# Paired first chunks, projection from columns, and the feature product behind the graph

## The chip, the cores and the metric

One core of a Trainium2 chip runs the whole program in one launch. The metric is device time in microseconds. The kernel before took 1318.92 us (median of three runs, 1317.95 to 1318.94).

## The reference

x is 4096x128, adj is 4096x4096 (values 0 or positive), all in fp32. Two layers follow each other, each with its residual and a layer norm over the 128 features.

```
A = adj without its diagonal, d = its diagonal
ns = A @ x                                   # node support
edge = gru(ns, x);  es = mean over 3 heads of gat(x, A)
node = gru(es, x)
x1 = layernorm(x + d * edge + d * node)
h2 = tanh(x1 @ W_proj + b_proj)
x2 = layernorm(x1 + relu(F @ (h2 @ W_gcn) + b_gcn)),  F = tanh(adj * adj) where adj > 0
```

A head of gat sums masked columns into scores, takes a softmax over each row of A and multiplies it by A and by x @ W. The top 350 entries of a row of F are all its entries here, since a row holds far fewer.

## The kernel before

The columns are cut into 8 chunks of 512, each chunk into 8 pieces: four 128x512 tiles of the transposed adjacency, 1 MB. All big products have their result in columns (features on the 128 partitions, 512 nodes on the free axis). Each engine runs its list of instructions in the written order; semaphores (wait_ge) tie them. Three stages follow each other.

**Support stage** (lines 130 to 520). The sync engine (SP) loads pieces into a ring of 5, and a load waits until TensorE, VectorE (mask) and ScalarE (sign count) are through with the piece five earlier. In chunk 0 each piece has its 256 KB of x loaded ahead of it, and the whole 2 MB of transposed x follows piece 7. TensorE makes ns (L427): four fp32 products a piece. Every fp32 product of the kernel stands in the trace as two records.

**Middle stage** (L1450 to L1830). For each of 256 tiles n (chunk c, k from 0 to 31): VectorE and ScalarE make gaps (L1723, L1614), ScalarE one exponential over three heads (L1621), VectorE the product with the adjacency (L1737), TensorE three products (L1821). Six buffers hold such terms. ScalarE's order in iteration n is gap(n+1), exp(n), and then what stands there for this n. At k = 8 TensorE combines the heads of the chunk before (L1788), and ScalarE takes that out at k = 12 (L1603).

**Tail** (L963 to L1443). For each chunk the gates of both cells run on TensorE (L1313, L1315: twelve 512-column products), ScalarE reads them (L1083, L1087, L1091) and makes n (L1095), VectorE makes the cells (L1175 to L1191) and adds them (add_cells, L1198). TensorE turns the sum into rows (turn_cells, L1324); VectorE multiplies by the diagonal and adds x (make_y, L1204), measures (L1211, L1214), GpSimd computes the inverse root (L1043 to L1055), VectorE normalizes (finish_x, L1218). TensorE turns the rows back (turn_x, L1332), multiplies by W_proj (project, L1339), ScalarE applies tanh (make_h2, L1107), TensorE multiplies by W_gcn (features, L1346), ScalarE copies (L1111). Then the graph product runs over 64 pieces: VectorE squares a piece (square_a, L1226), ScalarE takes tanh (L1115), TensorE does four products (graph, L1374). Three of the squares stand inside the gate chunks (0, 3 and 5). A chunk's features leave over ScalarE's relu (L1122), transposes (turn_features, L1385), VectorE's addition (L1236) and the second norm. The last 128 columns are done apart, in row form (L1371), with a single VectorE step behind them (L1232). Orders of the tail before:

```
ACT, chunk c: read_hid e, read_r e, read_z e, [tanh], h2(c-3), make_n e, read_hid n, read_r n, copy_x(c-2), read_z n, make_n n, copy_g(c-3)
DVE, chunk c: pre_n e, finish_x(c-2), make_y(c-1), measure(c-1), cell e, [square], pre_n n, cell n, add_cells(c)
PE,  chunk c: gates e, project(c-3), turn_cells(c-1), gates n (turn_x(c-2) inside), features(c-3)
```

Of the kernel before, what the change touches and what calls it, by code (L numbers as in the profile page):

```python
# [73 lines left out]

def piece_of(n):


    c, g = divmod(n, NPIECE)
    return c, (g + {0: 1, NCHUNK - 1: NCHUNK - 1}.get(c, 0)) % NPIECE
# [8 lines left out]
def loads_of(n):  # L88


    return 16 * (n // RING + (1 if n % RING else 0))


def wait_piece(engine, loaded, cleared, n):

    c, g = piece_of(n)
    if g == c:
# [41 lines left out]
def support_phase(nc, sem, dram, keep):  # L139
# [6 lines left out]
    x_ready = [sem(f"a_x{s}") for s in range(RING)]  # L146
    exps, parts_made, small = sem("a_exps"), sem("a_parts"), sem("a_small")
    loaded = [sem(f"a_loaded{s}") for s in range(RING)]
    first_loaded = [sem(f"a_first_loaded{j}") for j in range(PIECE)]
# [7 lines left out]
    with ExitStack() as ctx:  # L157
# [33 lines left out]

        def sync_program(sp):
            for n in range(NPIECE):
                tiles = slice((n + 1) % NPIECE * PIECE, ((n + 1) % NPIECE + 1) * PIECE)
# [4 lines left out]
                sp.dma_start(x_sb[:, tiles, :], dram["x_p"][:, tiles, :]).then_inc(x_ready[n % RING], 16)  # L199
                if n:  # L200
                    load_piece(sp, dram, pieces, loaded, n)
                else:
                    for j in range(PIECE):
                        sp.dma_start(pieces[:, 0, j, :], dram["adj_c"][0, :, PIECE + j, :]).then_inc(first_loaded[j], 16)
                if n == UV_AFTER:
                    sp.dma_start(x_t, dram["x_t"]).then_inc(x_t_ready, 16)
            for n in range(NPIECE, NPIECES):
                sp.wait_ge(masked, n - RING + 1)
                sp.wait_ge(signed, n - RING + 1)
                sp.wait_ge(ns_done, n - RING + 1)  # L210
                load_piece(sp, dram, pieces, loaded, n)
# [12 lines left out]
        def scalar_program(act):  # L224
            def count_below(n):
                if n:
                    wait_piece(act, loaded, cleared, n)
# [5 lines left out]
            def ns_take_out(c):  # L233
                b, out = c % 2, ns_sb[c % 2][:, :] if c < NCHUNK - 1 else last_ns
                act.wait_ge(ns_done, NPIECE * (c + 1))
# [14 lines left out]

            for j in range(PIECE):
                act.wait_ge(first_loaded[j], 16)
# [7 lines left out]
            for n in range(NPIECES):  # L260
                count_below(n)
                c, g = divmod(n, NPIECE)
                if c and g == 0:
                    ns_take_out(c - 1)
                if c and g == 2:
# [10 lines left out]
        def vector_program(dve):  # L276
            nc.vector.memset(ones[:, :], 1.0).then_inc(filled, 1)
            nc.vector.memset(wide_ones[:, :], 1.0).then_inc(filled, 1)
            nc.vector.memset(uv_parts[:, :, :], 0.0).then_inc(filled, 1)
            nc.vector.memset(w6[:, :], 0.0).then_inc(folded_out, 1)  # L280
            dve.wait_ge(filled, 3)
            nc.vector.memset(uv_parts[:, :, 0:1], 1.0).then_inc(filled, 1)

            def make_mask(n):
                c, g = piece_of(n)
                if n:
                    wait_piece(dve, loaded, cleared, n)
                else:
                    for j in range(PIECE):
                        dve.wait_ge(first_loaded[j], 16)  # L290
# [24 lines left out]
            for n in range(MASKS_FIRST):  # L315
                make_mask(n)
                if n == UV_AFTER - 2:
                    dve.wait_ge(folded, 1)
                    dve.wait_ge(folded_out, 1)
                    nc.vector.tensor_copy(w6[:, 0:NUV], w6_ps).then_inc(folded_out, 1)  # L320
                if n == UV_AFTER:
# [15 lines left out]
            for n in range(MASKS_FIRST, NPIECES):  # L337
                make_mask(n)
                c, g = divmod(n, NPIECE)
                if c and g == (4 if c < NCHUNK - 1 else NPIECE - 2):  # L340
                    make_e(c - 1)
# [74 lines left out]
        def tensor_program(pe):  # L416
            def ns_products(n, first=0, end=PIECE):
                c, g = piece_of(n)
                at = n % NPIECE
                if at == 0 and first == 0 and c >= 2:  # L420
                    pe.wait_ge(ns_out, c - 1)
                if n:
                    wait_piece(pe, loaded, cleared, n)
                for j in range(first, end):
                    if n == 0:
                        pe.wait_ge(first_loaded[j], 16)
# [5 lines left out]
            def pos_products(c, first=0, end=NPIECE):  # L432

                pe.wait_ge(masked, NPIECE * c + end)
# [4 lines left out]
                for i in range(first * PIECE, end * PIECE):  # L439
                    q, k = i % CHUNK, piece_of(NPIECE * c + i // PIECE)[1] * PIECE + i % PIECE  # L440
# [19 lines left out]

            for n in range(UV_AFTER + 1):
# [2170 lines left out]
```

## Time and profile before

| | |
|---|---|
| profiled execution | 1318.72 us, span 1317.1 us |
| support / middle / tail | 0 to 257, 257 to 981, 981 to 1317 us |
| PE / DVE / ACT / POOL busy | 99% / 77% / 71% / 8% |
| granted TensorE clock | 1.00 of full speed throughout |

The busy share says which engine has work nearly always. In the timelines, a record's "idle before" names what the engine waited for. TensorE's records overlap, so a stretch is best read from the start of one group to the start of the next.

### The profile page before, as it was taken

The page shows a single profiled execution, that of the slowest core. Times are in us where ns is not written, and L with a number is a line of the kernel's source. Part 1 is how long each engine was busy: PE and PEld are TensorE (multiplying, and loading weights), DVE is VectorE, ACT ScalarE, POOL GpSimd, SP SyncE. Part 2 cuts the span into 40 slices and gives each one's busy share as a digit, 9 for nine tenths or more (in the row PEclk, how much of TensorE's full clock was granted, in tenths as well). Part 3 has the DMA queues.
Part 4 walks back from the last instruction along what each step waited for, and adds up shares of the span by engine and source line. Part 5 has one row for each costly group of instructions (what it writes and reads, how often), then busy time and mean ns, then how long its engine had stood idle before and what let it go on. Part 6 is the DMA issues. An engine that isn't in the chain of part 4 may idle for free.

```text
span 1317.1 us, 12199 instructions
## 1 busy us (share of the span) xinstructions
PE 1304.8 (99%) x4203; PEld 590.0 (45%) x4203; DVE 1009.5 (77%) x1427; ACT 936.3 (71%) x950; POOL 102.5 (8%) x188
## 2 busy tenths in 40 slices
PE   8999999999999999999999999999999999999998
PEld 3444444444444444444444444444444555444445
DVE  2433333457998998999989999899868988678885
ACT  4655555338988899889889899898945556545563
POOL 0100001000100100100100100100003562000000
PEclk9999999999999999999999999999999999999999
DMA  9988888263233242232323423322113437888880
GB/s 367 355 291 287 281 296 295 79 238 127 84 139 130 95 146 96 97 143 97 145 99 116 152 96 122 118 96 96 64 62 129 144 115 252 296 307 294 302 285 18
DMA packets 46712, 228.95 MB, mean 174 GB/s; under 512 B 10611, under 2 KB 16436, under 8 KB 21044
## 3 DMA queue, kind: packets, MB, share of 16 engines
q1 hardware_dynamic: 44082, 225.55, 48.6%
q10 hardware_dynamic: 2562, 2.56, 0.6%
q8 instruction: 35, 0.57, 0.2%
q14 instruction: 33, 0.27, 0.1%
HBM read 223.80 MB, written 4.29 MB: 173 GB/s over the span
## 4 chain that ended last, share of the span: by engine, by line
PE 96%; DMA 2%; DVE 1%; issue 0%; SPq 0%; POOL 0%; ACT 0%; POOLq 0%
PE t_y_ps L1821 49%; PE ns_ps L427 15%; PE t_y_ps L1374 13%; PE rows_ps L1374 4%; PE t_y_ps L1799 3%; PE t_y_ps L1313 3%; PE t_y_ps L1315 2%; DMA pieces<-in_adj_c 2%; PE t_es_ps L1788 2%; PE pos_ps L441 1%; PE rows_ps L1315 1%; PE t_y_ps L1371 1%; PE t_es_ps L1346 1%; PE t_y_ps L1339 1%; DVE mask L1737 0%
## 5 line engine op out<-in xcount | busy, mean ns | idle before, releaser
L1821 PE MATMUL t_y_ps<-mask,x_sb 128*128 128x512 f32 x1536 | 662.6, 592 | 0.2 <-DVE mask L1737 0.2
L1821 PEld LDWEIGHTS t_y_ps<-mask,x_sb 128*128 128x128 f32 x1536 | 290.6, 190 | 366.0 <-issue 350.0
L1737 DVE TENSOR_TENSOR mask<-mask 128x1536 f32<-128x1536 f32 x256 | 450.1, 1759 | 0.2 <-ACT mask L1621 0.2
L1621 ACT ACTIVATE mask<-mask,ones 128x1536 f32<-128x1536 f32 x256 | 399.7, 1562 | 0.0
L1614 ACT ACTIVATE mask<-mask,pieces 128x512 f32<-128x512 f32 x352 | 241.5, 712 | 35.0 <-PE t_y_ps L1821 32.8
L427 PE MATMUL ns_ps<-pieces,x_sb 128*128 128x512 f32 x504 | 226.5, 602 | 6.8 <-DMA pieces<-in_adj_c 6.6
L1723 DVE TENSOR_SCALAR mask<-mask,e_cols 128x512 f32<-128x512 f32 x416 | 189.0, 487 | 50.6 <-PE t_y_ps L1821 44.2
L1115 ACT ACTIVATE mask<-mask 128x2048 f32<-128x2048 f32 x64 | 121.7, 1909 | 80.5 <-DVE mask L1226 80.0
L1374 PE MATMUL t_y_ps<-mask 128*128 128x512 f32 x384 | 167.0, 592 | 0.1
L427 PEld LDWEIGHTS ns_ps<-pieces,x_sb 128*128 128x128 f32 x504 | 93.8, 192 | 123.0 <-issue 116.6
L291 DVE TENSOR_SCALAR mask<-pieces 128x2048 fp8e4<-128x2048 f32 x64 | 76.8, 1224 | 93.1 <-DMA pieces<-in_adj_c 75.2
L1226 DVE SCALAR_TENSOR_TENSOR mask<-mask 128x2048 f32<-128x2048 f32 x64 | 142.2, 2282 | 0.8 <-DMA mask<-in_adj_c 0.8
L230 ACT ACTIVATE signs<-pieces 128x2048 fp8e4<-128x2048 f32 x64 | 122.3, 1911 | 26.2 <-DMA pieces<-in_adj_c 12.5
L1374 PEld LDWEIGHTS t_y_ps<-mask 128*128 128x128 f32 x384 | 72.3, 190 | 87.8 <-issue 86.6
L1575 POOL TENSOR_TENSOR mask<-mask,off_diag 128x128 f32<-128x128 f32 x32 | 30.8, 991 | 686.0 <-DMA mask<-in_adj_c 686.0
L1374 PE MATMUL rows_ps<-mask 128*128 128x512 f32 (+1 forms) x128 | 48.8, 539 | 0.0
L1313 PE MATMUL t_y_ps<-pieces 128*128 128x512 f32 x96 | 46.5, 593 | 0.0
L305 DVE TENSOR_SCALAR e_scl<-e_ps 128x128 f32<-128x128 f32 x8 | 2.3, 291 | 54.0 <-PE e_ps L453 54.0
L1799 PE MATMUL t_y_ps<-mask,pieces 128*32 128x512 fp8e4 x768 | 42.5, 379 | 0.0
L1236 DVE TENSOR_TENSOR x_sb<-t_y_ps,x_sb 128x512 f32<-128x512 f32 (+1 forms) x8 | 5.4, 675 | 42.1 <-PE t_y_ps L1385 42.1
L1374 PEld LDWEIGHTS rows_ps<-mask 128*128 128x128 f32 x128 | 24.2, 190 | 23.3 <-issue 15.1
L241 ACT COPY ns_sb<-ns_ps 128x512 f32<-128x512 f32 x7 | 4.1, 583 | 41.2 <-PE ns_ps L427 41.2
(177 smaller groups left out, 614.5 us busy)
## 6 DMA issues: line engine op xcount, KB each, us to landing
mask<-in_adj_c SPq DMA_DIRECT2D x128, 1024.0 KB, 4.8
pieces<-in_adj_c SPq DMA_DIRECT2D x63, 1024.0 KB, 5.0
mask<-scratch_shifts SPq DMA_DIRECT2D x8, 1536.0 KB, 7.3
x_sb<-in_x_p SPq DMA_DIRECT2D x8, 256.0 KB, 9.9
mask<-in_x_t SPq DMA_DIRECT2D x1, 2048.0 KB, 16.8
pieces<-in_x_t SPq DMA_DIRECT2D x8, 256.0 KB, 3.0
pieces<-scratch_ns_t SPq DMA_DIRECT2D x8, 256.0 KB, 3.6
scratch_ns_t<-ns_sb ACTq DMA_DIRECT2D x7, 256.0 KB, 5.9
```

What stands on the lines that cost most here:

```text
L230: nc.scalar.activation(signs[:, :], pieces[:, n % RING, :, :].rearrange("p k n -> p (k n)"), ACT.Relu, scale=-1.0, saturate=False, accum_o ...
L427: mm = nc.tensor.matmul(ns_ps[c % 2][:, :], x_sb[:, g * PIECE + j, :], pieces[:, n % RING, j, :], start=at == 0 and j == 0, stop=at == NPI ...
L1115: nc.scalar.activation(piece(u), piece(u), ACT.Tanh).then_inc(filtered, 1)
L1226: nc.vector.scalar_tensor_tensor(piece(u), piece(u), 0.0, piece(u), ALU.max, ALU.mult).then_inc(squared_a, 1)
L1313: mm = nc.tensor.matmul(gate_ps[g][:, :], whh[k][:, at:at + H], x_t[c % 2], start=True, stop=g == "hid_n")
L1374: mm = nc.tensor.matmul(f_ps[i % len(f_ps)][:, q * P:end * P], g_all[:, k, :], piece(u)[:, j * CW + q * P:j * CW + end * P], start=k == 0, ...
L1614: last = nc.scalar.activation(term(n)[:, h, :], shift_of(c)[:, 0, h, :], ACT.Relu, bias=minus_e[:, k, 1 + h:2 + h])
L1621: nc.scalar.activation(t, t, ACT.Exp, bias=ones[:, :], scale=-1.0).then_inc(exped, 1)
L1723: last = nc.vector.tensor_scalar(term(n)[:, h, :], shift_of(c)[:, 0, h, :], e_cols[:, k, 1 + h:2 + h], 0.0, ALU.subtract, ALU.max)
L1737: nc.vector.tensor_tensor(term(n), term(n), a, ALU.mult).then_inc(terms, 1)
L1799: mm = nc.tensor.matmul(sums_ps[g % 2][s * LINES:(s + 1) * LINES, :], parts[:, k, h, :], mask[:, c, k, :], start=k == 0, stop=k == NB - 1)
L1821: mm = nc.tensor.matmul(y_ps[c % 2][h][:, :], x_sb[:, k, :], term(n)[:, h, :], start=k == 0, stop=k == NB - 1)
```

## The change

**Head.** The pieces of chunks 0 and 1 come in pairs, (0,2), (1,2), (0,3), (1,3) and so on, the four with the diagonals last; a 256 KB part of x goes with each piece of chunk 0 only. The first two pieces are loaded and consumed by tile, the first part of x goes on ScalarE's queue, and transposed x comes in eight parts, one each behind pieces 8 to 15. TensorE begins with seven products of zeros. The scores' uv product stands behind piece 16, and pos_products, sum_e and turn_e of chunks 0 and 1 inside chunk 2.

**Tail.** The sum of the cells is multiplied by the diagonal and x is added while still in columns (make_y); that tile is turned into rows for the norm and also projected directly, with W_proj centered beforehand (center_weights, at tile (5, 10) of the middle stage, read out there by ScalarE). The norm's root and b_proj come in afterwards (scale_h). turn_x, copy_x and features go away. The graph product takes h2, and the product with W_gcn stands behind it (feed, in turn_features' place), the bias and relu with it on VectorE. The last 128 columns take this same way. The diagonal is loaded as rows, chunk by chunk; SP loads the first two ahead of the tail's first pieces and waits for all 24 y_scaled.

```
ACT, chunk c: read_hid e, read_r e, read_z e, [tanh], make_n e, read_hid n, copy_rows(c-1), read_r n, h2(c-2), read_z n, make_n n
DVE, chunk c: pre_n e, scale_h(c-2), measure_y(c-1), cell e, [square], pre_n n, cell n, make_y(c)
PE,  chunk c: gates e, turn_cells(c-1), gates n (project(c-1) inside)
```

```diff
+FIRST = [(c, g) for g in range(2, NPIECE) for c in range(2)] + [(c, g) for c in range(2) for g in range(2)]
+X_WITH = [n for n, (c, g) in enumerate(FIRST) if c == 0]
...
+    if n < len(FIRST):
+        return FIRST[n]
...
-UV_AFTER = NPIECE - 1
+BY_TILE = 2
+WARM = 7
+UV_AFTER = 2 * NPIECE
...
+            for n in range(NPIECES):
...
+                if n in X_WITH and n:
+                    load_x(sp, n)
+                if n >= BY_TILE:
                     load_piece(sp, dram, pieces, loaded, n)
                 else:
                     for j in range(PIECE):
...
+                if NPIECE <= n < NPIECE + NCHUNK:
+                    cols = slice((n - NPIECE) * CW, (n - NPIECE + 1) * CW)
+                    sp.dma_start(x_t[:, cols], dram["x_t"][:, cols]).then_inc(x_t_ready, 16)
...
+            load_x(act, 0)
...
+            pe.wait_ge(filled, 1)
+            zeros = uv_parts[:, :, :].rearrange("p t j -> p (t j)")
+            for i in range(WARM):
+                nc.tensor.matmul(e_t_ps[:, :], zeros[:, 0:P], zeros[:, 0:CW], start=True, stop=True)
...
+CENTER_AT = (5, 10)
...
+        nc.vector.tensor_scalar(center, ident[:, :], 1.0 / H, None, ALU.subtract).then_inc(bias_step, 1)
...
+        nc.tensor.matmul(bank[:, 0:H], center, w_proj, start=True, stop=True).then_inc(centered, 1)
...
+        act.wait_ge(centered, 1)
+        nc.scalar.copy(w_center, bank[:, 0:H]).then_inc(center_out, 1)
...
+        def copy_rows(c):
+            act.wait_ge(turned, c + 1)
+            nc.scalar.copy(x1[:, rows(c), :].rearrange("p r f -> p (r f)"), cell_ps[c % 2][:, :]).then_inc(rows_copied, 1)
...
+            act.wait_ge(scaled, CHUNK * (c + 1))
+            nc.scalar.activation(g_all[:, rows(c), :].rearrange("p r f -> p (r f)"), pre_h[c % 2], ACT.Tanh).then_inc(copied, 1)
...
             make_n("edge", c)
             read_hid("node", c)
+            if c:
+                copy_rows(c - 1)
             read_r("node", c)
             if c >= 2:
-                copy_x(c - 2)
+                make_h2(c - 2)
...
+            nc.vector.tensor_tensor(both, cell["edge"], cell["node"], ALU.add).then_inc(y_step, 1)
...
+            nc.vector.tensor_tensor(both, both, diag_rows[c % 2], ALU.mult).then_inc(y_step, 1)
...
+            nc.vector.tensor_tensor(both, both, x_t[c % 2], ALU.add).then_inc(cells, 1)
+
+        def scale_h(c):
+            dve.wait_ge(rooted, POOL_STEPS * (c + 1))
+            dve.wait_ge(projected, c + 1)
...
+                nc.vector.scalar_tensor_tensor(pre_h[c % 2][:, q * P:(q + 1) * P], h_ps[c % 2][:, q * P:(q + 1) * P], root[:, t:t + 1], b_proj,
+                                               ALU.mult, ALU.add).then_inc(scaled, 1)
...
+        def measure_y(c):
+            dve.wait_ge(rows_copied, c + 1)
+            measure(rows(c), stats, moments, stats_made, averaged)
...
             pre_n("edge", c)
             if c >= 2:
-                finish_x(c - 2)
+                scale_h(c - 2)
             if c:
-                make_y(c - 1)
-                measure(rows(c - 1), stats, moments, stats_made, averaged)
+                measure_y(c - 1)
             make_cell("edge", c)
...
+            if g == 3:
+                finish_x(c - 1)
...
+                mm = nc.tensor.matmul(h_ps[c % 2][:, q * P:(q + 1) * P], both[:, q * P:(q + 1) * P], w_center, start=True, stop=True)
...
+                mm = nc.tensor.matmul(back_ps[i % 2][:, t * P:(t + 1) * P], feat_t[i % 2][:, t * P:(t + 1) * P], w_gcn,
+                                      start=i not in BIAS_FIRST, stop=True)
...
-            if c >= 3:
-                project(c - 3)
             if c >= 1:
                 turn_cells(c - 1)
             pe.wait_ge(es_out, c + 1)
...
-            sp.wait_ge(y_scaled, HEADS * (NCHUNK - 1))
+            sp.wait_ge(y_scaled, HEADS * NCHUNK)
+            for c in range(2):
+                load_diag(sp, c)
             sync_tail(sp)
...
+                if (c, k) == CENTER_AT:
+                    keep_center(act, rows_ps)
...
+                    if (c, k) == CENTER_AT:
+                        pe.wait_ge(shifts_out, NGROUP)
+                        center_weights(pe, rows_ps)
```

## Rows read from the trace of the kernel before

**Rows 1.** The page: busy time of the engines, and the costliest group.
```profile
PE 1304.8 (99%) x4203; PEld 590.0 (45%) x4203; DVE 1009.5 (77%) x1427; ACT 936.3 (71%) x950; POOL 102.5 (8%) x188
...
L1821 PE MATMUL t_y_ps<-mask,x_sb 128*128 128x512 f32 x1536 | 662.6, 592 | 0.2 <-DVE mask L1737 0.2
```

**Rows 2.** Timeline (start, length, engine, line), the first 45 us, TensorE.
```profile
4.77 6.15 PE L427 MATMUL ns_ps<-pieces,x_sb 128*128 128x512 f32 x8 [4.77 <-DMA pieces<-in_adj_c]
12.73 14.38 PE L427 MATMUL ns_ps<-pieces,x_sb 128*128 128x512 f32 x32 [1.80 <-DMA pieces<-in_adj_c]
...
34.84 3.67 PE L427 MATMUL ns_ps<-pieces,x_sb 128*128 128x512 f32 x8 [0.20 <-POOL pieces L222]
```

**Rows 3.** Timeline, chunk 5 around tile 10 of the middle stage, ScalarE and VectorE.
```profile
742.66 1.56 ACT L1621 ACTIVATE mask<-mask,ones 128x1536 f32<-128x1536 f32 x1
...
752.33 0.59 ACT L1603 COPY mask<-t_es_ps 128x512 f32<-128x512 f32 x1 [2.84 <-PE t_es_ps L1788]
752.82 1.33 ACT L1614 ACTIVATE mask<-mask,pieces 128x512 f32<-128x512 f32 x2
...
755.71 1.75 DVE L1737 TENSOR_TENSOR mask<-mask 128x1536 f32<-128x1536 f32 x1
```

**Rows 4.** Windows (length, busy by engine, clock, DMA share, GB/s), a gate stretch.
```profile
1050.00:1100.00 50.00, 50.00 (x169) 26.02 (x168) 40.92 (x94) 25.61 (x37) 28.85 (x60) 1.00 0.45 160
```

**Rows 5.** Timeline, one chunk of the gates, VectorE.
```profile
1061.49 0.69 DVE L1180 SCALAR_TENSOR_TENSOR pieces<-pieces,rows_ps 128x512 f32<-128x512 f32 x1
1062.09 1.11 DVE L1218 TENSOR_SCALAR x_sb<-x_sb,h_moments,h_root 128x128 f32<-128x128 f32 x4
1063.12 1.12 DVE L1204 SCALAR_TENSOR_TENSOR x_sb<-t_y_ps,diag,x_sb 128x128 f32<-128x128 f32 x4
...
1065.34 0.66 DVE L1187 TENSOR_TENSOR pieces<-pieces 128x512 f32<-128x512 f32 x1
...
1073.50 0.69 DVE L1180 SCALAR_TENSOR_TENSOR pieces<-pieces,rows_ps 128x512 f32<-128x512 f32 x1 [0.41 <-PE rows_ps L1315]
```

**Rows 6.** Timeline, the same chunk, TensorE's turn_cells.
```profile
1061.16 0.60 PE L1324 MATMUL t_y_ps<-ident,pieces 128*128 128x128 f32 x4
```

**Rows 7.** Timeline, the same chunk, ScalarE.
```profile
1062.60 0.72 ACT L1095 ACTIVATE pieces<-pieces,h_bias 128x512 f32<-128x512 f32 x1
1063.21 0.69 ACT L1083 ACTIVATE pieces<-t_y_ps,h_bias 128x512 f32<-128x512 f32 x1
```

**Rows 8.** Timeline, first and last steps of the gates, SP's queue and VectorE.
```profile
981.50 1.28 SPq L1060 DMA_DIRECT2D mask<-in_adj_c  x3
...
981.58 1.89 DVE L1711 TENSOR_TENSOR mask<-t_y_ps,mask 128x512 f32<-128x512 f32 x3 [7.96 <-PE t_y_ps L1821]
...
986.29 2.29 DVE L1226 SCALAR_TENSOR_TENSOR mask<-mask 128x2048 f32<-128x2048 f32 x1 [0.79 <-DMA mask<-in_adj_c]
...
998.79 0.68 DVE L1175 SCALAR_TENSOR_TENSOR pieces<-pieces 128x512 f32<-128x512 f32 x1
...
1084.10 0.69 DVE L1198 TENSOR_TENSOR pieces<-pieces 128x512 f32<-128x512 f32 x1
```

**Rows 9.** Timeline, from the last gate to the steady graph product.
```profile
1091.32 0.36 DVE L1214 BATCH_NORM_AGGREGATE h_moments<-h_stats 128x2 f32<-128x6 f32 x4
...
1099.86 1.11 DVE L1218 TENSOR_SCALAR x_sb<-x_sb,h_moments,h_root 128x128 f32<-128x128 f32 x4 [3.80 <-POOL h_root L1055]
...
1106.36 1.90 ACT L1115 ACTIVATE mask<-mask 128x2048 f32<-128x2048 f32 x1
...
1108.40 16.98 PE L1374 MATMUL t_y_ps<-mask 128*128 128x512 f32 x39
```

**Rows 10.** Timeline, the end.
```profile
1294.80 0.67 ACT L1122 ACTIVATE pieces<-t_y_ps,pieces 128x512 f32<-128x512 f32 x1
...
1296.32 0.69 DVE L1236 TENSOR_TENSOR x_sb<-t_y_ps,x_sb 128x512 f32<-128x512 f32 x1 [3.36 <-PE t_y_ps L1385]
...
1312.14 0.29 DVE L1232 SCALAR_TENSOR_TENSOR x_sb<-t_y_ps,x_sb 128x128 f32<-128x128 f32 x1 [2.33 <-PE t_y_ps L1371]
```

More of the change, by code:

```diff
@@ L474, in tensor_program @@
             last.then_inc(uv_t_done, 1)
-            for n in range(UV_AFTER + 1, NPIECE + 1):
-                ns_products(n)
+            ns_products(UV_AFTER + 1)
             pe.wait_ge(uv_t_out, 2)
@@ L913, in load_small @@
                                  ).then_inc(keep["small_loaded"], 16)
+        if not diagonal:
+            return
         engine.dma_start(keep["diag"][:, :], dram["adj"].rearrange("a b -> (a b)")[0:N * N:N + 1]
@@ L1277, in vector_tail @@
             make_cell("node", c)
-            add_cells(c)
+            make_y(c)
         end = NCHUNK - 1
-        finish_x(end - 1)
+        scale_h(end - 1)
         square_a(3)
-        make_y(end)
-        measure(rows(end), stats, moments, stats_made, averaged)
+        measure_y(end)
         square_a(4)
         square_a(5)
-        finish_x(end)
+        scale_h(end)
         for u in range(6, NPIECE):
@@ L1291, in vector_tail @@
             c, g = divmod(u, NPIECE)
+            if g == 3:
+                finish_x(c - 1)
+            if c == end and g == 6:
+                finish_x(end)
             if c < end and g == 5:
@@ L1403, in tensor_tail @@
             gate("node", "r", c)
-            if c >= 2:
-                turn_x(c - 2)
+            if c == 1:
+                pe.wait_ge(center_out, 1)
+                pe.wait_ge(es_out, NCHUNK)
+            if c >= 1:
+                project(c - 1)
             gate("node", "z", c)
             gate("node", "in_n", c)
-            if c >= 3:
-                features(c - 3)
         end = NCHUNK - 1
-        project(end - 2)
         graph(0, 0)
@@ L1414, in tensor_tail @@
         turn_cells(end)
-        turn_x(end - 1)
-        features(end - 2)
-        graph(2, 0)
-        project(end - 1)
-        graph(3, 0)
-        features(end - 1)
-        graph(4, 0)
-        turn_x(end)
-        graph(5, 0, tiles=range(0, 2))
         project(end)
-        graph(5, 0, tiles=range(2, PIECE))
-        features(end)
-        end = (NCHUNK - 1) * NPIECE
-        for u in range(6, end):
+        for u in range(2, end * NPIECE):
             c, g = divmod(u, NPIECE)
@@ L1431, in tensor_tail @@
             if c and g == 2:
-                turn_features(c - 1)
-        for u in range(end, NPIECES):
-            graph(u, NCHUNK - 1, 0, CHUNK - 1)
-            if u == end + 4:
-                turn_features(NCHUNK - 2)
-        for u in range(end, NPIECES):
-            graph(u, NCHUNK, CHUNK - 1, CHUNK)
-            if u == end + 1:
-                turn_features(NCHUNK - 1)
-    return load_weights, load_in, make_biases, sync_tail, pool_tail, scalar_tail, vector_tail, tensor_tail
+                feed(c - 1)
+        last = len(END_PARTS) - 1
+        for u in range(end * NPIECE, NPIECES):
+            graph(u, end, 0, CHUNK - 1)
+            if u == end * NPIECE + 4:
+                feed(end - 1)
+        bias_first(last)
+        for u in range(end * NPIECE, NPIECES):
+            graph(u, last, CHUNK - 1, CHUNK)
+            if u == end * NPIECE + 1:
+                feed(end)
+        feed(last)
+    return load_weights, load_in, load_diag, make_biases, center_weights, keep_center, sync_tail, pool_tail, scalar_tail, vector_tail, tensor_tail
 def on_dve(k):
```

291 lines of the change are left out of this document (137 added, 154 removed).

## The prediction

> **What bounds the kernel now.** I read the page first: TensorE is busy 99% of the span, at 0.43 us a record (662.6 us over 1536) [rows 1], so a change gains what it takes off TensorE, unless it makes TensorE wait. Then the timelines, stretch by stretch, for how far the other engines are ahead. The reader is to see three places. At the start TensorE waits for loads: its first eight records take 6.15 us where eight later take 3.67, the second piece starts at 12.73, the next four pass at about 3.6 us each, and only from 34.84 is it never starved [rows 2]. In the middle stage ScalarE is four tiles ahead [rows 3], a lead that hides any short stop. In the gates TensorE is full, 50.0 of 50.0 us [rows 4], but VectorE waits for it only 0.41 us in a chunk of 12.01 us, from 1061.49 to 1073.50 [rows 5]: there the two are level, and work added to VectorE is not free.
>
> The sum is made against the profiled execution, 1318.7 us, 0.2 below the median of the runs.
>
> **Head.** A piece needs 8 records, 3.44 us, on TensorE. Before, each came with 1.25 MB, at 3.6 us a piece. In pairs it is 1.125 MB, 3.25 us at the same rate: TensorE becomes the slower one from the third piece. That piece lies behind 3.5 MB and not 3.75 MB of loads. Two pieces end now at 12.73 + 3.6 = 16.3; the third could be multiplied at about 15.5, and some 0.5 us earlier because the first x goes on another queue: 15.0. Then five pieces (17.2) and the small folding product (0.7) put the eighth at 32.9, against 34.84 [rows 2]: -1.9. Bounds: -0.5, if tile loads (eight issues ahead of the third piece) eat the lead, and -4, if only TensorE's own two pieces at full rate limited it. The seven products of zeros run while nothing has landed, at no cost, and spare the first pieces the slow rate; that is inside -1.9, since the second piece's landing decides. The transposed x, 0.25 MB behind each of eight pieces, is covered: a load is issued five pieces (17 us) ahead of its use. Moved pos_products, sum_e and turn_e are the same instructions with as many pieces around them: 0.
>
> **Middle: one step with one wait.** center_weights is 2 records of 128 columns, 0.22 us at four records in 0.44 (the length of the turn less its drain, 0.60 - 0.16) [rows 6]. But keep_center stands at the same tile (5, 10) in ScalarE's list as the product in TensorE's, and ScalarE waits for it. ScalarE's exponential of tile 170 ends at 744.22; the copy L1603, which stands behind the exponential of tile 172, waited 2.84 us for the combination behind tile 168 and did so without harm, as four tiles lay ready [rows 3]. TensorE ends that combination at 752.3, tiles 169 and 170 at 752.3 + 2 x 2.58 = 757.4, the centering at 757.7. Only now does ScalarE copy (0.3), make two gaps of tile 172 (1.24 from start to start of what follows [rows 3]), and the exponential of tile 171 (1.56); VectorE multiplies (1.75) [rows 3]; with hand-overs of 0.05 TensorE gets tile 171 at 762.7. All buffers have run dry: 5.0 us idle and 0.2 for the product, and 0.1 for the thin lead behind it: +5.3. Queued behind the waiting ScalarE instruction are all its gaps and exponentials, so both other engines stop. Bounds: 0.2, if ScalarE were less far ahead than counted, and 6.
>
> The trace shows TensorE's first eight records at 6.15 us instead of 3.44, behind an idle start, though the granted clock reads 1.00 of 2.4 GHz [rows 2, 4]. A second idle stretch of 5 us could bring that rate back: 6.15 - 3.44 = 2.7 us more. The Trainium skill (TensorE: Matmul & The Clock Gate, Why this matters for your kernels) says that a long enough gap between bursts of matmuls brings half rate back; by it the total would be 2.7 higher. No gap in this trace is long enough to test it.
>
> **Start of the tail.** SP now waits for VectorE's last scaling, 981.58 + 1.89 = 983.5, where the first pieces went out at about 981.5, and issues two broadcasts of the diagonal first: the first piece goes out 2.9 us later. VectorE's square of it stands between two gate steps at 986.29, when it landed [rows 8]; it comes at about 989.2, less 0.5 that VectorE already waited behind it for TensorE: +2.4. With two more additions to make_y of chunk 0, chunk 1 starts not at 998.79 but 3.0 to 3.9 later; the node half finds TensorE's results ready and takes back nearly 1: +2.9.
>
> **Gates.** TensorE loses turn_x (0.44), features (8 records of 128 columns, 0.89) and swaps project's two long records (0.86) for eight short (0.89): 12.93 us a chunk become 11.6, 1.3 x 8 = 10.4 us less. VectorE decides instead. Its chunk is 12.01 - 0.41 = 11.60. Out go finish_x (1.03) and the old make_y (about 1.15), together with measure (1.07) the stretch from 1062.09 to 1065.34 [rows 5]. In come scale_h, four instructions with a PSUM operand as the old make_y (1.15), and two 512-column operations more (0.69 each, 0.72 apart: 1.44): 12.0. Then a new wait. measure_y needs copy_rows, which needs the turn, which needs make_y, VectorE's last step of the chunk before. Count from the first pre_n: scale_h ends at 2.5. The turn is done at 0.8, but in ScalarE's list copy_rows stands behind make_n of the edge cell, which VectorE releases at 1.4 (two steps of 0.7), and read_hid: 1.44 + 0.61 [rows 7] + 0.58 = 2.6, copy 0.6 (as L1603 [rows 3]), so 3.25: VectorE waits 0.8. The chunk is 12.8, in chunk 1 too, which has no scale_h to fill the wait. The squares of chunks 3 and 5 (2.2 net of overlap each) lie on VectorE as before. Seven chunks: 7 x 12.8 + 4.4 = 94.0 against 1084.79 - 998.79 = 86.0 [rows 8]: +8.0. With +2.9 the last cell is made at 1095.7, 10.9 late, and TensorE waits about 1 us a chunk in turn_cells, with the node gates queued behind it. Bounds for the gates: -10.4 (all of TensorE's saving) to +12.
>
> **From gates to graph.** From 1095.7: scale_h(6) 1.15, square 2.2, tanh 1.9, copy_rows(7) 0.6 behind it, measure 1.1: 1102.7. GpSimd's root took 1099.83 - 1091.68 = 8.1 [rows 9]: 1110.8. scale_h(7) 1.15, square of piece 6 2.3, its tanh 1.9: 1116.2, while TensorE did pieces 0 to 5 from 1090.9 on. Before, piece 6 started at 1108.40 [rows 9]: +7.8. From there TensorE (3.44 a piece) is the slower again: VectorE has 2.2 a piece, and about 25 us in 27.9 a chunk; the later finish_x and bias additions (1.1 + 0.7) bring that to 27.
>
> **End.** feed has two records a tile where the transposes had one: 31 x 0.11 = 3.4, and the last tile. That one is on the path: after the graph's last product VectorE started at once at 1312.14; now ScalarE copies 128 columns (0.3; 0.67 is 512 of them [rows 10]), TensorE multiplies, VectorE follows. Relu to addition took 1296.32 - 1294.80 = 1.52 for four tiles [rows 10], so about 0.95 for one: +1.0. The bias row's product only changes place. Tail in all: 7.8 + 3.4 + 1.0 = 12.2.
>
> The copy stands behind a square root here. The Trainium skill (ScalarE: Activation LUTs, Table sets: the hidden batching unit) has copy in every table set, thus no reload; if not, two loads would be added. No row shows a copy behind a square root.
>
> **Sum.** 1318.7 - 1.9 + 5.3 + 12.2 = 1334.3; with the 0.2 to the median 1334.5 us.
>
> **Rivals.**
> (1) TensorE alone decides: the gates keep their VectorE slack and ScalarE's stop is hidden. -1.9 + 0.2 - 10.4 + 3.4 + 1.0 = -7.7: 1311.2 us, faster. For it: TensorE is 99% busy [rows 1] and loses 7 us net. Against: VectorE waited for it only 0.41 us a chunk [rows 5]. Should the stop at (5, 10) remain, it is 1316.3. It decides if VectorE's chunk is under 11.6.
> (2) Tail as forecast, the stop hidden (5.1 less): 1329.4. Against: ScalarE's tile 171 cannot start before the copy.
> (3) The stop as forecast, but copy_rows ready in time, seven times 0.8 less: 1328.9.
> (4) The forecast and half rate after the stop: 1337.2, the slowest of them. For it, the first records' rate [rows 2].
>
> **Chances.** Forecast 0.45; (1) in both forms 0.1; (2) 0.08; (3) 0.12; (4) 0.25. The range 1326 to 1341 holds all but the first, with errors of a few us in the counted waits. A change under 0.2% (2.6 us) is about what a measurement can't tell from none: faster 0.09, same 0.03, slower 0.88.
>
> **What would show it.** TensorE idle about 5 us behind tile (5, 10), released by VectorE's L1737 behind an exponential behind the center copy. VectorE idle 0.8 us a chunk ahead of bn_stats, released by ScalarE's copy; gate chunks of 12.8 us; turn_cells with TensorE idle ahead of it. Piece 6 of the graph about 8 us later than the head and middle shifts give. The eighth piece 2 us earlier. The prediction is wrong if TensorE stays full through (5, 10), or if gate chunks come at 11.6 to 12.

## The result, and the profile after

The changed kernel takes 1345.41 us (median of 5 runs, 1344.19 to 1348.10), the kernel before 1317.95 (5 runs beside it): a ratio of 1.0209, 95% interval 1.0198 to 1.0220. It is slower, as forecast, but 10.9 us slower than the forecast of 1334.5 and outside its range. The profiled execution of it took 1348.1 us, the slowest of the five; its span is 1346.8, 29.7 longer than before. Of the executions in the experiments one, of experiment 10, took 2322.54 us at a mean clock of 0.557; without it that kernel's median is 1337.95 us, with it 1338.17. I take the profiled span apart from start to end.

**Head.** Timeline of TensorE, start:

```profile
1.45 3.10 PE L492 MATMUL e_t_ps<-uv_parts 128*128 128x512 bf16 x7 [1.45 <-DVE ones L306]
5.19 7.21 PE L455 MATMUL ns_ps<-pieces,x_sb 128*128 128x512 f32 x16 [0.64 <-DMA x_sb<-in_x_p]
13.78 10.57 PE L455 MATMUL ns_ps<-pieces,x_sb 128*128 128x512 f32 x24 [1.37 <-DMA pieces<-in_adj_c]
24.18 0.73 PE L500 MATMUL end_ps<-a_sb,w_t 128*128 128x2 f32 x6
24.77 11.40 PE L455 MATMUL ns_ps<-pieces,x_sb 128*128 128x512 f32 x26
```

The seven products of zeros (L492) end before the first load is there. Two pieces are done at 12.4, the third starts at 13.78, and from there TensorE is full, the small folding product (L500) included: the eighth piece is reached at 24.77 + 16 x 0.43 = 31.7 where it was 34.84 [rows 2]. The whole stage stays 3.4 us ahead.

**Middle.** ScalarE, VectorE and TensorE around tile (5, 10), then windows (length, busy by engine, granted clock, DMA share, GB/s):

```profile
754.32 0.27 ACT L1095 COPY pieces<-rows_ps 128x128 f32<-128x128 f32 x1 [13.48 <-PE rows_ps L1091]
...
757.31 1.76 DVE L1773 TENSOR_TENSOR mask<-mask 128x1536 f32<-128x1536 f32 x1 [9.11 <-ACT mask L1655]
...
759.12 6.46 PE L1857 MATMUL t_y_ps<-mask,x_sb 128*128 128x512 f32 x11 [4.84 <-DVE mask L1773]
```
```profile
758.00:760.00 2.00, 0.88 (x1) 0.50 (x2) 2.00 (x4) 2.00 (x3) 0.00 (x0) 0.67 0.00 0
760.00:762.00 2.00, 2.00 (x4) 0.83 (x3) 1.92 (x2) 2.00 (x3) 0.00 (x0) 0.50 0.92 291
762.00:764.00 2.00, 2.00 (x6) 0.93 (x5) 1.44 (x1) 2.00 (x3) 0.00 (x0) 0.97 0.55 234
```

ScalarE stood 13.48 us ahead of a copy of 0.27, its lead of four tiles [rows 3] was gone, and TensorE waited 4.84 us. Then the granted clock fell to 0.50, which is 1.2 GHz, and TensorE lost another 1.6 us. The stage costs 6.8.

**Start of the tail and gates.** SP's queue and VectorE at the start; then TensorE in the gates of chunk 4, and the windows of that stretch:

```profile
986.95 0.80 SPq L1068 DMA_DIRECT2D mask<-in_diag  x2
987.79 1.52 SPq L1120 DMA_DIRECT2D mask<-in_adj_c  x3
```
```profile
994.98 2.29 DVE L1282 SCALAR_TENSOR_TENSOR mask<-mask 128x2048 f32<-128x2048 f32 x1 [6.07 <-DMA mask<-in_adj_c]
...
1007.22 0.68 DVE L1220 SCALAR_TENSOR_TENSOR pieces<-pieces 128x512 f32<-128x512 f32 x1
```
```profile
1041.14 1.88 PE L1372 MATMUL t_y_ps<-pieces 128*128 128x512 f32 x4
...
1049.64 1.11 PE L1383 MATMUL t_y_ps<-ident,pieces 128*128 128x128 f32 x4 [3.19 <-DVE pieces L1249]
1050.55 3.62 PE L1372 MATMUL t_y_ps<-pieces 128*128 128x512 f32 x4
```
```profile
1049.00:1051.00 2.00, 1.36 (x5) 1.25 (x6) 1.97 (x4) 0.05 (x1) 0.00 (x0) 0.50 0.13 39
1051.00:1053.00 2.00, 2.00 (x3) 0.67 (x2) 0.95 (x4) 1.11 (x2) 0.00 (x0) 0.50 0.85 277
1053.00:1055.00 2.00, 2.00 (x4) 0.85 (x3) 1.25 (x9) 0.72 (x2) 0.01 (x1) 0.50 0.74 151
1055.00:1057.00 2.00, 2.00 (x12) 1.25 (x11) 1.93 (x4) 1.13 (x2) 1.82 (x3) 0.84 0.92 386
```

The first square starts at 994.98 where it was 986.29 [rows 8], and chunk 1 at 1007.22 where it was 998.79: 8.4 later, 5.0 of them made here. From 1007.22 the seven chunks and the last cell take until 1108.80, 101.6 us where they took 86.0: +15.6. A chunk without a square, with TensorE at full clock, takes 12.83 (1021.63 to 1034.46), as forecast. But behind the waits of 2.63, 3.19 and 3.17 us TensorE runs four records in 3.6 us instead of 1.88. The granted clock is at 0.50 for about 3 us in the first case and nearly 7 in the other two. As the node gates of that chunk lie in this stretch, VectorE waits for them: the chunks that begin so take 14.41, 15.67 and 15.69 us and not 12.83, together 7.3 us more. The other two long ones, 15.05 and 15.02, are the plain chunk and a square. In a second profile of the same kernel (experiment 9) the three chunks take 14.44, 14.08 and 14.41 us, together 4.4 more: the waits are the same, the price of the clock behind them is not.

**Graph and end.** TensorE:

```profile
1129.41 19.10 PE L1407 MATMUL t_y_ps<-mask 128*128 128x512 f32 x40 [2.22 <-ACT mask L1168]
...
1323.63 1.16 PE L1426 MATMUL t_y_ps<-pieces 128*128 128x128 f32 x8 [2.36 <-ACT pieces L1175]
1324.62 7.91 PE L1407 MATMUL rows_ps<-mask 128*128 128x384 f32 x24
...
1341.31 0.49 PE L1426 MATMUL t_y_ps<-pieces 128*128 128x128 f32 x2 [0.35 <-ACT pieces L1175]
```

Piece 6 starts 21.0 later than before [rows 9], less than the last cell (24.0 later), about as forecast. Its 40 records then take 19.10 and not 17.40, behind a wait of 2.22. The feeds cost 3.6 (0.45 for each of the first six, 0.55 and 0.34 for the two behind them). In the last chunk, whose records have 384 columns, TensorE waits 2.36 for VectorE, which costs 2.5, and the end is 0.9 longer. Head -3.4, middle +6.8, start +5.0, gates +15.6, up to piece 6 -3.0, from there +8.7: 29.7.

### The profile page after: what moved, and what is told of

Its sections match the earlier page's. It is cut to its first block, busy times and chain, and to the rows that moved or that the text cites. A ratio compares the mean times of both kernels' runs of the same rounds, so it can differ in the third digit from the quotient of the medians.

```text
span 1346.8 us, 12227 instructions
## 1 busy us (share of the span) xinstructions
PE 1312.2 (97%) x4197; PEld 591.9 (44%) x4197; DVE 1026.3 (76%) x1452; ACT 931.2 (69%) x944; POOL 97.5 (7%) x188
## 4 chain that ended last, share of the span: by engine, by line
PE 86%; DVE 8%; issue 2%; ACT 1%; DMA 1%; POOL 1%; SPq 0%; DVEq 0%; POOLq 0%; ACTq 0%
PE t_y_ps L1857 48%; PE ns_ps L455 16%; PE t_y_ps L1407 10%; PE t_y_ps L1835 3%; PE rows_ps L1407 3%; DVE mask L1282 2%; PE t_es_ps L1824 1%; PE pos_ps L469 1%; PE t_y_ps L1372 1%; DVE pieces L1225 1%; DMA pieces<-in_adj_c 1%; DVE mask L1773 1%; DVE pieces L1234 1%; PE t_y_ps L1426 1%; DVE pieces L1232 1%
## 5 line engine op out<-in xcount | busy, mean ns | idle before, releaser
L455 PE MATMUL ns_ps<-pieces,x_sb 128*128 128x512 f32 x504 | 223.4, 597 | 2.0 <-DMA pieces<-in_adj_c 1.4
L1407 PE MATMUL t_y_ps<-mask 128*128 128x512 f32 (+1 forms) x448 | 175.9, 552 | 4.3 <-ACT mask L1168 3.2
L253 ACT ACTIVATE signs<-pieces 128x2048 fp8e4<-128x2048 f32 x64 | 122.3, 1911 | 27.9 <-DMA pieces<-in_adj_c 11.6
L1407 PEld LDWEIGHTS t_y_ps<-mask 128*128 128x128 f32 x448 | 80.1, 192 | 95.4 <-issue 95.3
L1372 PE MATMUL t_y_ps<-pieces 128*128 128x512 f32 x96 | 51.7, 651 | 0.3 <-ACT pieces L1144 0.3
L1156 ACT ACTIVATE pieces<-pieces,h_bias 128x512 f32<-128x512 f32 x16 | 11.5, 721 | 34.9 <-DVE pieces L1225 34.9
L1291 DVE TENSOR_TENSOR mask<-t_y_ps,pieces 128x512 f32<-128x512 f32 (+1 forms) x8 | 5.4, 675 | 33.5 <-PE t_y_ps L1426 33.5
## 6 DMA issues: line engine op xcount, KB each, us to landing
mask<-in_x_t SPq DMA_DIRECT2D x8, 256.0 KB, 10.9
```

The source lines that it names most:

```text
L253: nc.scalar.activation(signs[:, :], pieces[:, n % RING, :, :].rearrange("p k n -> p (k n)"), ACT.Relu, scale=-1.0, saturate=False, accum_o ...
L455: mm = nc.tensor.matmul(ns_ps[c % 2][:, :], x_sb[:, g * PIECE + j, :], pieces[:, n % RING, j, :], start=at == 0 and j == 0, stop=at == NPI ...
L1407: mm = nc.tensor.matmul(f_ps[i % len(f_ps)][:, q * P:end * P], g_all[:, k, :], piece(u)[:, j * CW + q * P:j * CW + end * P], start=k == 0, ...
```

## The experiments

Each ran on one core beside the kernel before, whose median was 1318.8, 1318.0 and 1318.4 us in the three sets. "Less" below is against the changed kernel's 1345.41. One minus the mean granted clock, times the span, is an upper bound of what TensorE loses by the clock, since part of the low stretches lies in its waits: for the changed kernel (0.991 to 0.994 over nine runs) 8 to 12 us, for the kernel before (0.998 to 1.000) at most 3.

| kernel | median us | ratio to before, 95% | clock of the profiled run |
|---|---|---|---|
| head alone | 1315.74 | 0.9978, 0.9969 to 0.9987 | 1.000 |
| all but the head | 1348.40 | 1.0209, 1.0185 to 1.0233 | 0.992 |
| sums 4 tiles later | 1338.09 | 1.0146, 1.0131 to 1.0162 | 0.994 |
| statistics later | 1343.04 | 1.0186, 1.0170 to 1.0201 | 0.993 |
| products in the waits | 1342.96 | 1.0192, 1.0175 to 1.0209 | 0.996 |
| diagonal behind piece | 1340.76 | 1.0176, 1.0159 to 1.0193 | 0.997 |
| normalizing late | 1342.42 | 1.0181, 1.0164 to 1.0198 | 0.991 |
| no squares in gates | 1345.14 | 1.0208, 1.0191 to 1.0225 | 0.991 |
| changed, again | 1346.57 | 1.0214, 1.0197 to 1.0231 | 0.991 |
| transposes later | 1338.17 | 1.0145, 1.0125 to 1.0166 | 0.994 |
| four mends | 1329.72 | 1.0082, 1.0065 to 1.0099 | 1.000 |
| mends without added work | 1323.07 | 1.0044, 1.0024 to 1.0064 | 0.997 |

**1. The head alone.** The kernel before with the pieces in pairs, loads by tile, x on its own queue and the warm products; the middle and the tail as they were.

> The kernel before with the head's edits alone (pairs, loads by tile, first x on ScalarE's queue, transposed x in parts, seven products of zeros); the tail is as before. Theory: the head gains 3.4 us, as the two traces show at the combination of chunk 4 (749.56 before, 746.17 after), and nothing behind it gives that back: 1318.0 - 3.4 = 1314.6. Rival: the later stages are paced by something else (loads, ScalarE), and the lead is lost on the way: 1318.

1315.74 us, 3.1 less than the kernel before beside it where 3.4 were expected: a gain of 0.2%, small but outside the interval, and the only version that is faster than the kernel before.

**2. All but the head.**

> The kernel before with the tail's edits alone (centering at tile (5, 10) included). Theory: the two halves add, so this is the changed kernel without the head's gain: 1345.4 + 3.4 = 1348.8. Rival: the halves meet (the tail's waits depend on where the head leaves the queues), and it is elsewhere by more than 1.5 us.

1348.40 us. The two parts add (1348.4 - 3.1 = 1345.3); nothing of the slowdown comes from the head. One of the four runs took 1341.22 us at a mean clock of 0.998, where the others have 0.992 to 0.994: what this tail loses by the clock varies between executions of one program.

**3. ScalarE takes the sums out four tiles later.**

```diff
-                if (c, k) == CENTER_AT:
+                if (c, k) == (CENTER_AT[0], CENTER_AT[1] + 4):
```

> The changed kernel with ScalarE taking out the centered weights at tile (5, 14) instead of (5, 10); TensorE makes them at (5, 10) as before. Theory: the stop of 4.84 us goes, and with it the half rate of TensorE behind it (1.6 us): 1345.4 - 6.6 = 1338.8. Rival A, without an effect of the clock: the stop alone, 4.9 less, 1340.5. Rival B: the lead of ScalarE is too thin there anyway and the stop comes elsewhere: 1345.

1338.09 us, 7.3 less than the changed kernel, and the stretch has neither the wait nor the low clock:

```profile
740.00:780.00 40.00, 40.00 (x96) 17.73 (x95) 35.88 (x39) 35.78 (x38) 0.00 (x0) 1.00 0.30 105
```

The middle's cost is wholly the place of one copy. The four runs spread from 1335.75 to 1340.65 us, so it is the trace and not the median that speaks against rival A.

**4. Statistics behind the edge's cell.**

```diff
-            if c:
-                measure_y(c - 1)
             make_cell("edge", c)
+            if c:
+                measure_y(c - 1)
```

> The changed kernel with measure_y behind the edge cell on VectorE, so that the copy of the rows is there when it is wanted. Theory: 0.8 us go in each of seven chunks, 2.4 instead in chunk 1, and the half rate behind chunk 1's wait with it (about 1.6): 1345.4 - 5 x 0.8 - 2 x 1.8 - 2.4 - 1 = about 1335 to 1338; half rate behind chunks 3 and 5 stays, since the square still holds VectorE 2.2 us there. Rival: VectorE then waits as long for TensorE's node gates, which are queued behind the turn: no change, 1345.

1343.04 us, 2.4 less where 7 to 10 were expected. VectorE in a plain chunk:

```profile
1027.44 0.87 DVE L1264 BATCH_NORM_STATS2 h_stats<-x_sb 128x6 f32<-128x128 f32 x4
...
1028.50 0.66 DVE L1220 SCALAR_TENSOR_TENSOR pieces<-pieces 128x512 f32<-128x512 f32 x1
1029.98 0.69 DVE L1225 SCALAR_TENSOR_TENSOR pieces<-pieces,rows_ps 128x512 f32<-128x512 f32 x1 [0.82 <-PE rows_ps L1374]
```

The wait for the copy is gone and stands a few instructions later, ahead of the same chunk's second L1225, as a wait for TensorE's node in_n, which is queued behind the transposes. The chunk takes 12.73 (1023.03 to 1035.76). The expectation had named that rival.

**5. More work for TensorE in the long waits.**

```diff
+                if c - 1 in FILTERED_IN:
+                    if c >= 3:
+                        pe.wait_ge(rows_copied, c - 2)
+                    for _ in range(3):
+                        nc.tensor.matmul(cell_ps[(c - 1) % 2][:, :], whh["edge"][:, 0:H], x_t[c % 2], start=True, stop=True)
                 turn_cells(c - 1)
```

> The changed kernel, and ahead of the transposes of the cells that follow a chunk with a square (chunks 0, 3 and 5) three more products 128x512 of the edge's weights by x, into the bank that the transposes then overwrite: 3 x 0.86 = 2.6 us of work for TensorE, in the stretches in which it stood idle 2.63, 3.19 and 3.17 us for VectorE. It is nothing but more work. Theory (a stretch of over two idle us is followed by some microseconds at half clock, and that, not the wait itself, is the larger part of what the gates cost beyond the forecast): the stretch stays as long, but the 2 us behind each stay at a granted clock of 1.0, the four transposes and four records behind take 0.66 + 1.88 us and not 1.11 + 3.62, and the kernel gains up to 7.3 us: 1338.5 us (1337 to 1341). Rival (the slow stretch has another cause, such as contention with the square or what VectorE hands over): no change, 1345.4. Rival (the added products delay the transposes): 1346 to 1348.

TensorE ahead of chunk 4, to be held against the rows of the changed kernel above:

```profile
1044.19 2.74 PE L1444 MATMUL t_y_ps<-pieces 128*128 128x512 f32 x6
1047.54 0.66 PE L1383 MATMUL t_y_ps<-ident,pieces 128*128 128x128 f32 x4 [0.61 <-DVE pieces L1249]
1048.03 1.88 PE L1372 MATMUL t_y_ps<-pieces 128*128 128x512 f32 x4
```

The transposes come at the same point of VectorE's work, and behind them the records pass at the full rate; no stretch of the gates has a clock under 1.00, and the chunks behind take 12.83 us. One trace alone would not show that the added work is the reason, since in experiment 6 the clock stayed up behind such waits in the profiled run. But the mean clocks of all four runs (0.995 to 0.997) lie above all nine of the changed kernel (0.991 to 0.994). The profiled run took 1340.49 us, the median is 1342.96: 2.5 to 3.6 us less than the changed kernel's two medians, not 7.3, and the intervals of the ratios overlap. The 7.3 was the price in one profile; in the second it is 4.4. And in the profiled run here the clock fell behind the wait of 2.36 in the last chunk instead, where 24 records took 9.60 us for 7.91.

**6. The diagonal's loads behind the first piece.**

```diff
+            if u == 0:
+                sp.wait_ge(y_scaled, HEADS * NCHUNK)
+                for c in range(2):
+                    load_diag(sp, c)
...
-            sp.wait_ge(y_scaled, HEADS * NCHUNK)
-            for c in range(2):
-                load_diag(sp, c)
-            sync_tail(sp)
+            sp.wait_ge(y_scaled, HEADS * (NCHUNK - 1))
+            sync_tail(sp, y_scaled)
```

> The changed kernel, with the two broadcast loads of the diagonal's rows (128x512 each, from 2 KB) issued behind the first adjacency piece of the tail and not ahead of it. Theory (they hold the DMA engines for some 4 us, at 140 to 260 GB/s where a piece comes at 330 and more, and the first square waits 6.07 us for its piece at 994.98): the piece lands 2 to 4 us earlier, and the whole tail starts so much earlier, 1342 to 1343.5 us. Rival (the square hides behind the inverse root chain, or its place is taken by another wait, for a load of x or ns): 1345.4.

1340.76 us, 4.7 less, more than expected. VectorE waits 0.89 and not 6.07 for the piece, and chunk 1 starts 3.6 earlier, counted from the last scaling. The 1.5 us that it is still later than before are make_y's two more operations in chunk 0. TensorE:

```profile
1004.72 0.66 PE L1387 MATMUL t_y_ps<-ident,pieces 128*128 128x128 f32 x4 [0.89 <-DVE pieces L1253]
...
1045.41 0.66 PE L1387 MATMUL t_y_ps<-ident,pieces 128*128 128x128 f32 x4 [3.18 <-DVE pieces L1253]
1045.91 1.88 PE L1376 MATMUL t_y_ps<-pieces 128*128 128x512 f32 x4
```

The first long wait has become a short one. And here, behind the same 3.18 idle us as in the changed kernel, four records take 1.88: the clock did not fall. That is this execution, 1336.49 us at a mean clock of 0.997; the other three took 1340.75 to 1341.97 us at 0.992 to 0.995, so they lost more by the clock.

**7. The last normalizings behind the last square.**

```diff
-            if g == 3:
+            if c < end and g == 3:
                 finish_x(c - 1)
-            if c == end and g == 6:
-                finish_x(end)
...
+        finish_x(end - 1)
+        finish_x(end)
         add_x1(end - 1)
```

> The changed kernel, with the normalizing of x for the last two chunks (2 x 1.11 us on VectorE) moved out of the squares of the last chunk to behind its last square, where VectorE stood idle 3.67 us for the feed. Theory (in the last chunk a piece is 384 columns a tile, TensorE is through with it sooner than VectorE squares the next, and those 2.2 us end as the 2.36 us for which TensorE waits at 1323.63): the wait falls to 0.1 to 0.3, 1343.2 us (1342.8 to 1343.8). Rival (the ring's loads or ScalarE's tanh set the rate there): 1345.4, and the wait stays.

1342.42 us, 3.0 less; the wait at the last chunk's feed falls from 2.36 to 0.32:

```profile
1319.80 1.16 PE L1426 MATMUL t_y_ps<-pieces 128*128 128x128 f32 x8 [0.32 <-ACT pieces L1175]
```

**8. Two squares taken out of the gates.** `FILTERED_IN = {0: 0}`, pieces 1 and 2 squared behind the last cell.

> The changed kernel with two squares (and their tanh) taken out of the gates of chunks 3 and 5 and put behind the gates, ahead of the third. By the sum of the prediction, in which VectorE's work is a chain and TensorE merely waits, it is no change: 2 x 2.2 us less in the gates, 4.4 us more between them and piece 6. By the theory of the clock: the gates of chunks 4 and 6 begin on stretches of 0.9 idle us instead of 3.2, keep the full clock, and lose 2 x (2.2 + 2.6) us, with 4.4 us back behind the gates: 1340.2 us (1339 to 1342.5); if the longer wait behind the gates costs half a clock of its own, up to 1344.

1345.14 us: no change, as by the forecast's sum, against my theory's 1340.2. But that sum has no half clock in it, and this run has (mean 0.991), so the agreement does not bear it out. TensorE behind the gates:

```profile
1093.76 3.67 PE L1411 MATMUL t_y_ps<-mask 128*128 128x512 f32 x8 [1.06 <-DVE pieces L1227]
1104.28 5.29 PE L1411 MATMUL t_y_ps<-mask 128*128 128x512 f32 x8 [6.85 <-ACT mask L1168]
```

The gates of chunks 2 to 7 do run at full clock in 12.83 us each and the graph's first piece starts 10.0 us earlier, but one wait of 6.85 follows, and eight records behind it take 5.29 for 3.67. A wait moved brings its slow stretch along. In this profile the clock also fell behind the wait of 2.36 us in the last chunk (1.7 us).

**9. The changed kernel again.**

> The changed kernel itself once more, nothing changed. Theory (of the stretches of 2.2 to 3.2 idle us in which TensorE waits in the tail, each is followed by half clock in some executions and not in others, so that the same program loses anything from none to 9 us there): 1343 to 1348, median 1345.4, a mean clock between 0.991 and 0.997, and the lost microseconds in other places than in the first profile or fewer of them. Rival (it is bound to the place): the same three gates and piece 6 again at 0.50.

1346.57 us, clock 0.991 to 0.993, and the low clock in the same places:

```profile
1049.00:1051.00 2.00, 1.23 (x5) 1.23 (x6) 1.94 (x4) 0.00 (x0) 0.05 (x1) 0.54 0.12 20
...
1081.00:1083.00 2.00, 2.00 (x3) 0.67 (x2) 1.12 (x7) 1.04 (x2) 0.00 (x0) 0.50 0.92 230
...
1129.00:1131.00 2.00, 2.00 (x4) 0.68 (x3) 2.00 (x2) 1.91 (x1) 0.00 (x0) 0.50 0.00 0
```

For these places the rival was right. But the size differs (4.4 us in the gates and not 7.3), and in the last chunk the clock fell behind the same wait of 2.36 us behind which it had stayed up in the first profile:

```profile
1320.92 1.16 PE L1426 MATMUL t_y_ps<-pieces 128*128 128x128 f32 x8 [2.36 <-ACT pieces L1175]
1321.91 9.60 PE L1407 MATMUL rows_ps<-mask 128*128 128x384 f32 x24
```

So the loss is regular in part only: one program, the same wait, 7.91 us for the 24 records in one execution and 9.60 in the other.

**10. Transposes behind the node gates hid_n and r.** With the edit of 4:

```diff
-            if c >= 1:
-                turn_cells(c - 1)
             pe.wait_ge(es_out, c + 1)
             gate("node", "hid_n", c)
             gate("node", "r", c)
+            if c >= 1:
+                turn_cells(c - 1)
...
             read_hid("node", c)
+            read_r("node", c)
             if c:
                 copy_rows(c - 1)
-            read_r("node", c)
```

> The changed kernel, with the transposes of the cells put behind the node gates hid_n and r (they stood ahead of them), ScalarE's copy of them behind the reading of r, and the statistics behind the edge's cell. Theory (VectorE's 12.83 us a chunk are 12.0 of work and 0.8 of waiting, for the copy; moving the statistics alone turned that into a wait for the gate in_n, because the node gates stood behind the transposes; with both moved neither wait is left): chunks without a square take 12.0 to 12.15 us, the gates end 5 to 5.6 us earlier, 1339.8 us (1338 to 1342). Rival (the copy comes late now, as it waits behind node hid_n and r and two readings on ScalarE): 12.8 us a chunk and 1345.4, or more.

1338.17 us, 7.2 less. VectorE's chunk takes 11.99 us, as the forecast had it for VectorE's work (12.0). Only the 0.79 us for ScalarE's n, which stands in every chunk, before too, is left in it:

```profile
1019.74 0.68 DVE L1220 SCALAR_TENSOR_TENSOR pieces<-pieces 128x512 f32<-128x512 f32 x1
...
1031.73 0.68 DVE L1220 SCALAR_TENSOR_TENSOR pieces<-pieces 128x512 f32<-128x512 f32 x1
```

TensorE's long waits in the gates are gone with it. One of 2.79 us stands ahead of the graph, and its first 16 records take 8.66 for 7.11; the clock also fell behind 2.25 ahead of piece 6 and 2.36 in the last chunk.

**11 and 12. The mends together.** Eleven: 3, 5, 6 and 7. Twelve: 3, 6, 7 and 10, no work added.

> The changed kernel with four of the mends at once: the column sums taken out four tiles later, the diagonal's loads behind the first piece, the last two normalizings behind the last square, and the extra products ahead of three chunks' transposes. If the terms add up: 1345.4 - 7.3 - 4.6 - 3.0 - 1.5 (what the products still gain once the first of the long waits is gone) = 1329.0 us (1327 to 1331.5), which leaves 11 us over the kernel before for the gates, the feeds and the end. If they hide one another: above 1333.

1329.72 us: the terms add up. The profiled run has no stretch of low clock while TensorE works. With the first long wait already shortened, the products ahead of chunk 1's transposes are in the way there: that chunk takes 14.19 us and not the 12.83 of experiment 6.

> The changed kernel with the mends that move work and add none: column sums four tiles later, diagonal's loads behind the first piece, last normalizings late, and transposes and statistics moved as in the run before. If the terms add up: 1345.4 - 7.3 - 4.6 - 3.0 - 5.6 = 1324.9 us (1323 to 1328). That would still be above the kernel with the head alone (1315.7), as six feeds (2.7 us), the longer end (1.5 us) and VectorE's chain behind the gates are left. Rival (the gates' mend is none): 1330.

1323.07 us, 1.8 below the expectation, and still 5 above the kernel before. TensorE in the profiled run (1321.23 us):

```profile
1079.89 10.13 PE L1411 MATMUL t_y_ps<-mask 128*128 128x512 f32 x16 [2.79 <-DVE pieces L1229]
...
1106.38 17.40 PE L1411 MATMUL t_y_ps<-mask 128*128 128x512 f32 x40 [1.29 <-ACT mask L1172]
```

Piece 6 starts 2.0 us earlier than before the change: 3.4 come from the head, and the tail up to there has lost 1.4, with 3.0 at half clock behind the wait of 2.79 in it. From there on it takes 4.8 us longer than before, nearly all of it the feeds and the end. One of the ten executions took 1335.35 us at a mean clock of 0.985, the others 1321.23 to 1324.18. The best version measured is the head alone, 1315.74.

## Why the prediction was wrong

Right were the direction and two mechanisms: VectorE becomes the bound of the gates, and ScalarE's copy stops the middle. By its steps, in the profiled executions (forecast 1334.3, measured 1348.1):

- **Head**, forecast -1.9, measured -3.4 in the changed kernel, -3.1 alone: the third piece could be multiplied at 13.78, not at 15.0. Its landing was put too late.
- **Middle stop**, forecast +5.3, measured +6.8: 4.84 idle for 5.0, and then 1.6 us at half clock. Rival (4) had the slow stretch, at 2.7.
- **Start of the tail**, forecast +2.9, measured +5.0. The forecast counted when the queue gets to the piece, and took the two broadcasts ahead of it as costless to the DMA engines. They took 3.3 and 5.2 us to land. The first 1 MB piece did go out 2.9 us later, as forecast, counted without the shifts before it, but then took 7.2 us from its issue at 987.79 to the square at 994.98, where it had taken 4.8. Experiment 6 removes 3.6 of the 5.0; the rest, 1.5, is make_y's two more operations, which the forecast had counted.
- **Gates**, forecast +8.0, measured +15.6. The forecast's chunk of 12.8 is there, 12.83, with the 0.80 wait for the copy. **This is the step that failed**: by the sum "TensorE waits about 1 us a chunk in turn_cells", at the price of the wait alone. In the chunks behind a square the wait is 2.6 to 3.2 us, and half clock behind it costs 7.3 us more in this profile, 4.4 in the second one (experiment 9). The forecast had the squares in the gates and added them to VectorE's chain, but never asked how long TensorE stands idle there; with 12.83 + 2.2 against 11.85 of TensorE's own work it is 3.2. The rival with half rate stood at one place only.
- **From the gates to piece 6**, forecast 3.1 less than the last cell's lateness, measured 3.0 less.
- **Feeds and end**, forecast 3.4 + 1.0, measured 3.6 + 0.9: right. To them came 1.7 at half clock behind the 2.22 wait, and 2.5 by the wait in the last chunk. That VectorE has "about 25 us in 27.9 a chunk", 27 with what is added, is an average; the last chunk has 384 columns a record, TensorE needs a quarter less for most pieces, VectorE as much as ever, and two normalizings lie in it. Experiment 7.

Half clock is 1.6 + 7.3 + 1.7 = 10.6 of the 13.8 us by which the profiled run misses the sum. This run is 2.7 us above the median; in the second profile, 1347.1 us, half clock comes to about 9.5 (1.7 in the middle, 4.4 in the gates, 1.7 ahead of piece 6 and 1.7 in the last chunk). The Trainium skill (TensorE: Matmul & The Clock Gate, Why this matters for your kernels) advises against longer idle gaps between bursts of matmuls in the middle of a kernel. The traces agree at 4.84 and 6.85 us, where the clock fell every time. But it fell behind most waits of 2.2 to 3.2 us as well, so that here waits shorter than the page's limit are at risk too; the measurement decides.

Rival (1), TensorE alone decides, named VectorE's chunk under 11.6 us as its condition. Experiment 10 measures 11.99 without any wait for TensorE, and before it was 12.01 with 0.41 of such waiting [rows 5]. The 1.3 us that TensorE saves in a chunk had no taker even in the best order: in experiment 12, chunks 1 to 6 take 76.0 us, before the change 73.6. So it pays the feeds and the end (4.5 us) for a saving that VectorE doesn't let through. Rival (2), the stop hidden, was not the case, as TensorE waited 4.84 us, nor rival (3), the copy in time: the copy took its 0.80.

The copy behind a square root reloads no table, as the prediction had it: ScalarE's last copy, at 1340.99, stands between two square roots (L1215, at 1337.95 and 1342.89), takes 0.27 us, and the timeline has no table load between them.

## What to carry to other kernels

Before taking work off the busiest engine, write down the length of the second engine's chain per step; if it is within a few per cent, the gain is nothing and the waits are new. Price a wait of TensorE of over 2 us at its length and 1.3 to 3.0 us more, wherever it stands, and take this second part as a risk and not as certain (it came behind 31 of the 42 such waits in these tails), and look at whole steps (the one with the extra square, the last one with fewer columns), not at averages. If a wait is moved and comes back under another name, look at what is queued behind the instruction that it stood on.

## What the runs showed of the hardware

In the tails of the twelve profiled runs of the changed kernel and its variants there are 42 waits of TensorE between 2.2 and 3.2 us. At the end of 31 of them, or just behind, the granted clock fell to 0.50 (1.2 GHz), and in the gates four records took 2.8 to 3.6 us for 1.88. Behind the other 11 it did not fall (numbers in brackets are experiments):

| wait, us | clock fell | did not |
|---|---|---|
| 3.17 to 3.19 | 10 | 2 (both in 6) |
| 2.79 | 2 (10, 12) | 0 |
| 2.62 to 2.63 | 7 | 0 |
| 2.36 | 4 (5, 8, 9, 10) | 5 (first profile, 2, 3, 4, 6) |
| 2.28 to 2.29 | 1 (4) | 1 (4) |
| 2.21 to 2.25 | 7 | 3 (5, 6, 11) |

It fell behind 4.84 us all nine times and behind 6.85 us the one time, and behind no wait of 1.3 us or less. The length of the wait alone does not decide: at 2.36 us it fell in one execution of the changed kernel and not in the other. In 5, 6 and 11 the first wait of the tail (2.63 us) had been filled or shortened; but that was so in 10 and 12 too, and there the clock fell behind the next, of 2.79. What decides was not found.

Two loads of 256 KB that spread a row of 2 KB over 128 partitions took 3.3 and 5.2 us to land. In slices of 0.4 us the DMA engines moved 118 to 261 GB/s during the first 3 us behind their issue, and then, with the 1 MB pieces, mostly 330 to 490.
